# Tile 1's first half of W without A's columns, tile 0's h inside it, and warm-up products that read a constant: one change to a 16-tile LoRA kernel

## What is computed

```python
x = x + einsum('bct,bcd->bdt', x, weights[itok_B_0_15])
base_out = einsum('bti,oi->bto', x, W) + b
lora_h = einsum('bti,bir->btr', x, lora_As[itok_B_0_23])
lora_out = einsum('btr,bro->bto', lora_h, lora_Bs[itok_B_0_23])
x = x + base_out + lora_out * SCALING
```

## Time and profile before

| what | us |
|---|---|
| median of 3 runs (lowest, highest) | 84.74 (84.66, 84.76) |
| profiled execution, its own time | 84.83 |
| its span in the trace | 83.0 |
| PE busy (matmuls) | 78.5 (94%) |
| DVE (VectorE) busy | 60.1 (72%) |
| ACT (ScalarE) busy | 52.4 (63%) |
| POOL (GpSimd) busy | 33.5 (40%) |

### The profile page before, as it was taken

One profiled execution on the slowest core, in us unless ns is written; L12 is line 12 of the kernel. 1 busy time (PEld: TensorE's weight loads), 2 busy tenths in 40 slices (PEclk: granted clock), 3 DMA queues, 4 the chain that ended last, 5 costly groups with the idle time before them and its releaser, 6 DMA issues.

```text
span 83.0 us, 2012 instructions
## 1 busy us (share of the span) xinstructions
PE 78.5 (94%) x524; PEld 71.2 (86%) x524; DVE 60.1 (72%) x158; ACT 52.4 (63%) x180; POOL 33.5 (40%) x75
## 2 busy tenths in 40 slices
PE   4999599999999999999999999999999999999970
PEld 2376498899999999999999999999999999999950
DVE  2049595877879787777878787978777777869560
ACT  1555758866666675958666666667685867665520
POOL 6108843744443517080715344352608071304300
PEclk9999999999999999999999999999999999999999
DMA  2899899998476766877668778667774626130334
GB/s 24 279 349 317 202 253 216 355 252 247 142 233 197 255 197 241 198 230 196 183 205 200 210 190 241 173 238 184 236 179 155 167 91 175 30 118 0 126 126 126
DMA packets 16141, 16.07 MB, mean 193 GB/s; under 512 B 10241, under 2 KB 10626, under 8 KB 16130
## 3 DMA queue, kind: packets, MB, share of 16 engines
q1 hardware_dynamic: 14016, 11.67, 46.9%
q0 software_dynamic: 1248, 4.06, 18.6%
q10 hardware_dynamic: 866, 0.21, 1.1%
HBM read 11.74 MB, written 4.19 MB: 192 GB/s over the span
## 4 chain that ended last, share of the span: by engine, by line
PE 85%; DMA 6%; ACTq 3%; ACT 2%; DVE 1%; issue 1%; DVEq 0%
PE z_ps L565 58%; PE z_ps L602 9%; DMA a_raw<-in_lora_a 6%; PE y_ps L617 4%; PE y_ps L615 4%; PE y_ps L613 4%; PE ht_ps L589 2%; ACTq L326 1%; PE ht_ps L652 1%; PE z_ps L597 1%; DVE y_sb L552 1%; ACT L320 1%; ACTq L316 1%; ACT a_sb L391 0%; ACTq L317 0%
## 5 line engine op out<-in xcount | busy, mean ns | idle before, releaser
L565 PE MATMUL z_ps<-wa,x_hi 128*128 128x288 f32 (+2 forms) x240 | 50.1, 301 | 0.0
L565 PEld LDWEIGHTS z_ps<-wa,x_hi 128*128 128x128 f32 x240 | 38.0, 188 | 1.8 <-issue 0.5
L565 PE MATMUL z_ps<-wa,x_lo 128*128 128x288 f32 (+2 forms) x120 | 35.3, 295 | 0.0
L565 PEld LDWEIGHTS z_ps<-wa,x_lo 128*128 128x128 f32 x120 | 22.6, 188 | 0.0
L303 POOL CAST m_hi<-m_raw 128x128 fp32r<-128x128 f32 x16 | 4.8, 301 | 35.3 <-ACT m_raw L340 35.3
L294 POOL DMA_INDIRECT b_raw<-in_lora_b,b_index_slot x16 | 16.8, 1048 | 4.4 <-POOL b_index_slot L292 4.4
L384 ACT CAST z_hi<-z_ps 128x256 fp32r<-128x256 f32 x31 | 10.1, 376 | 10.2 <-PE z_ps L602 10.1
L487 DVE TENSOR_TENSOR z_lo<-z_ps,z_hi 128x256 fp32r<-128x256 f32 x31 | 11.8, 420 | 6.3 <-ACT z_hi L384 6.3
L340 ACT COPY m_raw<-w_raw 32x32 f32 x64 | 13.8, 216 | 1.8 <-DVE w_raw L519 0.9
L446 DVE TENSOR_TENSOR x_lo<-x_raw,x_hi 128x512 fp32r<-128x512 f32 x14 | 9.7, 690 | 3.7 <-ACT x_hi L352 3.7
L467 DVE TENSOR_TENSOR b_lo<-b_raw,b_hi 128x512 fp32r<-128x512 f32 x15 | 10.4, 691 | 0.5
(11 more groups left out here) (58 smaller groups left out, 76.7 us busy)
## 6 DMA issues: line engine op xcount, KB each, us to landing
out<-y_sb SPq DMA_DIRECT2D x15, 256.0 KB, 2.4
x_raw<-in_xt SPq DMA_DIRECT2D x14, 256.0 KB, 3.2
a_raw<-in_lora_a SPq DMA_DIRECT2D x60, 32.0 KB, 2.9
first_sb<-in_first SPq DMA_DIRECT2D x2, 384.0 KB, 3.9
first_sb<-in_first SPq DMA_DIRECT2D x3, 256.0 KB, 4.8
b_raw<-in_lora_b,b_index_slot POOLq DMA_INDIRECT x16, 4.0
bias_sb<-in_bias SPq DMA_DIRECT2D x1, 256.0 KB, 4.3
a_raw<-in_lora_a ACTq DMA_DIRECT2D x4, 32.0 KB
```

The lines of the kernel that those rows point to most:

```text
L565: done = nc.tensor.matmul(target, (x_lo if lo_x else x_hi)[s][:, k, :], moving(lo_w), start=first and not lo_x and not lo_w, stop=last and ...
```

## The change

Five things change together. (1) The warm-up products read the program's constant of one (set up in the preamble) instead of a tile that VectorE clears, so they wait for nothing; the last has 384 columns in place of 256. (2) A is laid out on the host and in `a_raw` as [r][k], k innermost. Tile 0's h then reads its stationary operand straight from `a_raw` with a step of four elements, and the ScalarE copy is gone; but `round_a` and `rest_a` of every tile now read `a_raw` with that step too. (3) Tile 1 treats A as the last tile does: none beside half 0, 64 columns beside half 1. (4) Half 0 of tile 1 runs right after tile 0's chunks with waits cut finer, tile 0's h comes after its third chunk, and ScalarE and VectorE take W's last chunk ahead of tile 1's A. (5) `load_a(3)` waits for the end of tile 0's h on TensorE; and later tiles wait for z of the tile two back one half at a time.

```diff
-    WARM_UP = (512,) * 8 + (256,)
+    WARM_UP = (512,) * 8 + (384,)
...
-        a_raw = [sb(f"a_raw{s}", [P, J, KC, R], F32) for s in range(NA)]
-        a0_sb = sb("a0_sb", [P, KC, JR], F32)
+        a_raw = [sb(f"a_raw{s}", [P, J, R, KC], F32) for s in range(NA)]
...
+        def a0_chunk(k):
+            return a_raw[0][:, :, :, k:k + 1].rearrange("p j r a -> p (j r a)")
...
         def a_half(u, half):
-            return a_raw[u % NA][:, half * HJ:(half + 1) * HJ, :, :].rearrange("p j k r -> p k j r")
+            return a_raw[u % NA][:, half * HJ:(half + 1) * HJ, :, :].rearrange("p j r k -> p k j r")
+        WITH_A = {1: 1, LAST: 0}
         def a_place(u, half, lo):
-            row, at = (0, A_AT[1] + half * AC) if u == LAST else (half, A_AT[u % 2])
+            row, at = (WITH_A[u], A_AT[1] + half * AC) if u in WITH_A else (half, A_AT[u % 2])
...
                 if u == NA:
-                    sp.wait_ge(a0_ready, 1)
+                    sp.wait_ge(main_done, 1)
...
             round_x1(0)
-            act.wait_ge(a_loaded[0], 16 * J)
-            act.copy(a0_sb[:, :, :].rearrange("p k (j r) -> p k j r", j=J),
-                     a_raw[0][:, :, :, :].rearrange("p j k r -> p k j r")).then_inc(a0_ready, 1)
             round_x1(1)
+            round_w(KC - 1)
             round_a(1)
-            round_w(KC - 1)
...
             rest_x1(1)
+            rest_w(3)
             rest_a(1)
-            rest_w(3)
...
-            pe.wait_ge(zeros_ready, 1)
             for columns in WARM_UP:
+                nc.tensor.matmul(ht_ps[:, 0:columns], nc.const_aps.tensor(1.0, (P, P), BF16),
+                                 nc.const_aps.tensor(1.0, (P, columns), BF16), start=True, stop=True)
...
+            def half_chunk(u, k, half, parts=(HH, HL, LH)):
+                n = HALF + 2 * AC if half == WITH_A[u] else HALF
+                return products(u, k, z_ps[1][:, half, 0:n], lambda lo: wa[:, k, lo, half, AC:AC + n], parts)
             def main_chunk(u, k, half):
...
+                if k == 0 and half == 1:
+                    pe.wait_ge(z_ready, 2 * (u - 1))
...
             def wait_main(u):
-                pe.wait_ge(x_ready, u + (u > 1))
-                pe.wait_ge(a_ready, 2 * u - (u == 1))
-                if u >= 2:
-                    pe.wait_ge(z_ready, 2 * (u - 1))
+                pe.wait_ge(x_ready, u + 1)
+                pe.wait_ge(a_ready, 2 * u)
+                pe.wait_ge(z_ready, 2 * (u - 1) - 1)
...
+            def first_h():
+                pe.wait_ge(a_loaded[0], 16 * J)
+                for k in range(KC):
+                    last = nc.tensor.matmul(ht_ps[0:JR, 0:P], a0_chunk(k), x0_chunk(k), start=k == 0,
+                                            stop=k == KC - 1, skip_group_check=True)
+                last.then_inc(main_done, 1)
+            pe.wait_ge(x_hi_ready, 1)
+            for k in range(2):
+                pe.wait_ge(w_ready, k + 1)
+                half_chunk(1, k, 0, (HH, HL))
+            pe.wait_ge(x_ready, 1)
+            for k in range(2):
+                half_chunk(1, k, 0, (LH,))
+            pe.wait_ge(x_hi_ready, 2)
+            pe.wait_ge(w_ready, 3)
+            half_chunk(1, 2, 0, (HH, HL))
+            pe.wait_ge(x_ready, 2)
+            half_chunk(1, 2, 0, (LH,))
+            first_h()
+            pe.wait_ge(w_hi_ready, KC)
+            half_chunk(1, 3, 0, (HH, LH))
+            pe.wait_ge(w_ready, KC)
+            half_chunk(1, 3, 0, (HL,))
+            pe.wait_ge(a_ready, 2)
+            half_chunk(1, 0, 1)
+            half_chunk(1, 1, 1)
+            lora(0, 0)
+            lora(0, 1)
+            half_chunk(1, 2, 1)
+            half_chunk(1, 3, 1).then_inc(main_done, 1)
...
-        "lora_a": lora_a.reshape(-1, KC, P, R).transpose(0, 2, 1, 3),
+        "lora_a": lora_a.reshape(-1, KC, P, R).transpose(0, 2, 3, 1),
```

More of the change, by code:

```diff
@@ L26, in lora_residual_program @@
     C, S0, _ = w0.shape
-    SLOTS, _, _, R = lora_a.shape
+    SLOTS, _, R, _ = lora_a.shape
     T = KC * P
@@ L70, in lora_residual_program @@
         own_mask0 = sb("own_mask0", [JR, J, C], F32)
-        zeros = sb("zeros", [P, P], BF16)
         scratch = sb("scratch", [P, 1], F32)
@@ L119, in lora_residual_program @@
         last_part_stored = sem("last_part_stored")
-        zeros_ready = sem("zeros_ready")
         ident_zero = sem("ident_zero")
@@ L139, in lora_residual_program @@
         a_ready = sem("a_ready")
-        a0_ready = sem("a0_ready")
         b_hi_ready = sem("b_hi_ready")
@@ L179, in a_half @@
         def a_half(u, half):
-            return a_raw[u % NA][:, half * HJ:(half + 1) * HJ, :, :].rearrange("p j k r -> p k j r")
+            return a_raw[u % NA][:, half * HJ:(half + 1) * HJ, :, :].rearrange("p j r k -> p k j r")
+        WITH_A = {1: 1, LAST: 0}
         def a_place(u, half, lo):
-            row, at = (0, A_AT[1] + half * AC) if u == LAST else (half, A_AT[u % 2])
+            row, at = (WITH_A[u], A_AT[1] + half * AC) if u in WITH_A else (half, A_AT[u % 2])
             return wa[:, :, lo, row, at:at + AC].rearrange("p k (j r) -> p k j r", j=HJ)
         def h_of(u):
-            if u == LAST:
-                return z_ps[1][:, 0, HALF:HALF + 2 * AC].rearrange("p (a j r) -> p a j r", a=2, j=HJ)
+            if u in WITH_A:
+                return z_ps[1][:, WITH_A[u], HALF:HALF + 2 * AC].rearrange("p (a j r) -> p a j r", a=2, j=HJ)
             at = H_PS[u % 2]
@@ L230, in load_a @@
                     slot = sp.snap(adapters[j], min_val=0, max_val=SLOTS - 1)
-                    sp.dma_start(a_raw[u % NA][:, j:j + 1, :, :].rearrange("p j k r -> p j (k r)"),
-                                 lora_a[bass.ds(slot, 1)].rearrange("s p k r -> p s (k r)")
+                    sp.dma_start(a_raw[u % NA][:, j:j + 1, :, :].rearrange("p j r k -> p j (r k)"),
+                                 lora_a[bass.ds(slot, 1)].rearrange("s p r k -> p s (r k)")
                                  ).then_inc(a1_half_loaded[j // HJ] if u == 1 else a_loaded[u % NA], 16)
@@ L317, in _ @@
             act.dma_start(ids_p_sb[:, :], ids_of_p).then_inc(ids_p_loaded, 16)
-            act.wait_ge(zeros_ready, 1)
-            act.copy(scratch[:, :], zeros[:, 0:1])
+            act.copy(scratch[:, :], nc.const_aps.tensor(1.0, (P, 1), BF16))
             adapters0 = [act.alloc_register(f"adapter0_{j}") for j in range(J)]
@@ L325, in _ @@
                 slot = act.snap(adapters0[j], min_val=0, max_val=SLOTS - 1)
-                act.dma_start(a_raw[0][:, j:j + 1, :, :].rearrange("p j k r -> p j (k r)"),
-                              lora_a[bass.ds(slot, 1)].rearrange("s p k r -> p s (k r)")
+                act.dma_start(a_raw[0][:, j:j + 1, :, :].rearrange("p j r k -> p j (r k)"),
+                              lora_a[bass.ds(slot, 1)].rearrange("s p r k -> p s (r k)")
                               ).then_inc(a_loaded[0], 16)
@@ L430, in _ @@
         def _(dve):
-            nc.vector.memset(zeros[:, :], 0.0).then_inc(zeros_ready, 1)
             nc.vector.memset(own_mask[:, :], 0.0).then_inc(mask_zero, 1)
@@ L567, in products @@
+            HH, HL, LH = (0, 0), (0, 1), (1, 0)
+            def products(u, k, target, moving, parts=(HH, HL, LH)):
+                for part in parts:
+                    done = nc.tensor.matmul(target, (x_hi, x_lo)[part[0]][u % 2][:, k, :], moving(part[1]),
+                                            start=k == 0 and part == HH, stop=k == KC - 1 and part == parts[-1],
                                             skip_group_check=True)
                 return done
+            def half_chunk(u, k, half, parts=(HH, HL, LH)):
+                n = HALF + 2 * AC if half == WITH_A[u] else HALF
+                return products(u, k, z_ps[1][:, half, 0:n], lambda lo: wa[:, k, lo, half, AC:AC + n], parts)
@@ L570, in main_chunk @@
             def main_chunk(u, k, half):
                 s = u % 2
[L572 to L577, removed]
+                if k == 0 and half == 1:
+                    pe.wait_ge(z_ready, 2 * (u - 1))
                 return products(u, k, z_ps[s][:, half, 0:NW],
-                                lambda lo: wa[:, k, lo, half, MOV[s]:MOV[s] + NW], k == 0, k == KC - 1)
+                                lambda lo: wa[:, k, lo, half, MOV[s]:MOV[s] + NW])
@@ L649, in _ @@
                 first_chunk(k)
[L650 to L656, removed]
+            def first_h():
[28 more added lines that the diff above has]
+            half_chunk(1, 3, 1).then_inc(main_done, 1)
+            for u in range(2, LAST):
                 wait_main(u)
                 main_chunk(u, 0, 0)
[L660 to L664, removed]
+                main_chunk(u, 0, 1)
+                mix(u - 2)
+                transpose_h(u - 1)
+                main_chunk(u, 1, 0)
                 main_chunk(u, 1, 1)
@@ L673, in last_chunk @@
             def last_chunk(k, half):
-                n = (HALF + 2 * AC, HALF)[half]
```

(5 more changed lines are left out.)

## The result

| | before | changed |
|---|---|---|
| median of four runs, us | 84.75 | 87.0 |
| lowest and highest | 84.66, 84.77 | 86.46, 87.09 |
| profiled execution (span) | 84.83 (83.0) | 87.09 (85.4) |

What follows compares the result with a forecast made beforehand. PE looked saturated, busy 94%, with VectorE's masked h arriving at the same moment, without slack. Terms -0.65 + 0.22 + 0.1 + 2.64 = +2.3 us on 84.83 gave 87.1, as median 87.0; range 83.8 to 88.3.

Steps and rivals of the forecast that it cites:

- The read with a step: VectorE's rests of A read lone elements four apart: 110 ns more per rest, between nothing and 133.
- No slack in the loop: Two longer rests stand ahead of the masked h on VectorE: 0.22 us per tile, 12 x 0.22 = 2.64.
- The signs: Expected profile: tile of 4.70, PE idle some 0.2 us before LoRA products, DVE busier by 3.3, PE's busy time hardly changed.
- The start: Filled 0.88 us gap: tile 2 at about 14.1, tile 1's LoRA products 0.65 earlier; step adds 0.22 and 0.1.
- The warm-up: Earlier warm-up products before tile 0: counted at nothing, since tile 0's third chunk still waits for VectorE.
- The wait that is moved: A of tile 3 loads after tile 0's h, from 11.18; ScalarE waits for its landing, 15.65 at median.
- The bias behind A of tile 3: Bias queued behind those loads is needed a tile later; counted at nothing.
- rival with a free read: Stepped read of A costs nothing, so the start's 0.65 stays: 84.1, at best 83.8; chance 0.25.
- the late A: A of tile 3 lands late and the read is free: with 4.0 from issue, +0.4, 85.1; chance 0.06.
- the unmoved start: Tile 2 still begins at 15.00, the loop still pays: 84.74 + 2.64 = 87.4; inside the forecast's range, no separate chance.

Runs made afterwards that it cites:

- runs of two: Changed kernel with A of tiles 1 to 15 in runs of 2 neighbours instead of 16, masked h behind the rests; 84.84 us, measured once.
- masked h first: Changed kernel with VectorE's masked h put ahead of the two rests of A in tiles 2 to 14; 84.24 us, 0.9935 of the kernel before.
- both cures: Changed kernel with A of tiles 1 to 15 in runs of 16 and the masked h ahead of the rests of A; 84.18 us.
- both cures, four buffers: Changed kernel with A of tiles 1 to 15 in runs of 16, masked h ahead of the rests, and a fourth buffer for A; 84.12 us.
- layout undone: Changed kernel with A of tiles 1 to 15 laid out as before, only tile 0's A in the new layout; 84.48 us, 0.9956 of the kernel before.

## Why the prediction was right

The total, 87.0, was met, and the mechanism was the one forecast. Two terms were off, the start by 0.28 and the loop by 0.34, and cancelled; that the total fits so closely is luck, that the kernel is slower through VectorE's longer rests is not.

- *The read with a step.* Forecast 110 ns per rest, measured 377 - 284 = 93, or 0.73 ns for each of 128 elements, not the nearly full second element time that I took. The estimate from the Trainium skill (Vector Engine (DVE) Microarchitecture Reference, "Measured stream behaviour on trn2"), 87 ns, was nearer, although its price is for hops of 4 KiB and here a step is 16 bytes; its pairs at full rate agree with the 284 ns of runs of two.
- *No slack in the loop.* Forecast 12 x 0.22 = 2.64; measured 2.30, of which 0.30 fall in the first of the twelve periods (below) and 0.18 in each of the others. Two rests of 93 ns make 0.19: nearly their whole length passes through.
- *The signs.* A tile of 4.68 and a DVE busier by 2.8 us came near the 4.70 and 3.3 forecast. But PE showed no idle time ahead of the LoRA products, and its busy time rose by 3.3 us: the wait stands on PEld, 0.18 a tile, with the masked h as releaser.
- *The start.* Forecast -0.33 with the step's share in it, measured -0.05. Several steps failed here. The warm-up was counted at nothing, but tile 0's chunks ended at 9.17, not 8.51: PE's pace rose late in this execution (last section). Tile 0's h took 1.22, not 1.09: its weight loads read the stepped layout in 207 ns, before 136, and I had taken nothing. So M and z of tile 0 came later, z's rest at 14.36 and not 13.6 (before 14.10), and tile 2 began at 14.93, not 14.1. The loads of h, before and changed, and z's rest in the changed kernel:

```profile
L652 PEld LDWEIGHTS ht_ps<-first_sb,a_sb 128*64 128x64 f32 x8 | 0.8, 136 | 1.3 <-ACT a_sb L391 1.3
```

```profile
L652 PEld LDWEIGHTS ht_ps<-first_sb,a_raw 128*64 128x64 f32 x8 | 1.0, 207 | 0.1
```

```profile
14.36 0.76 DVE L484 TENSOR_TENSOR z_lo<-z_ps,z_hi 128x256 fp32r<-128x256 f32 x2 [0.78 <-ACT z_hi L385]
```

- *The wait that is moved.* In this execution the step failed in its reason. A of tile 3 was not what ScalarE waited for: its issues ran from 11.90, later than the 11.18 forecast, yet its casts show no wait, as the first two timelines below say. In two quicker starts (masked h first, both cures) ScalarE did wait for it, until 15.64 and 15.71, near the 15.65 forecast.
- *A of tile 4*, behind it in the same queue, has no term in the forecast. ScalarE waited 0.26 for it (the third timeline), the second rest of that tile started behind the late cast, and the first period of the loop took 4.78 where the others took 4.67: some 0.11 of the 2.30 go with this wait and not with the rests alone.

```profile
11.90 1.90 SPq L233 DMA_DIRECT2D a_raw<-in_lora_a  x4
```

```profile
15.63 0.76 ACT L367 CAST wa<-a_raw 128x128 fp32r<-128x128 f32 x2
```

```profile
20.78 0.74 ACT L367 CAST wa<-a_raw 128x128 fp32r<-128x128 f32 x2 [0.26 <-DMA a_raw<-in_lora_a]
```

- *The bias behind A of tile 3*, which I had counted at nothing, did wait in the quicker starts (0.75 us with the masked h first, 0.33 with both cures).
- The sum with measured terms: 84.83 - 0.05 + 2.30 = 87.08; the profiled execution took 87.09.

The rival with a free read fell with the 377 ns; the late A and the unmoved start fell as causes of the loss, since undoing the layout alone gave 84.48. Of the late A the 0.11 above is left, and the rival of the unmoved start describes this start well: z of tile 0 came no earlier and tile 2 began 0.07 earlier, although the reason, the late rise of the pace, stands in no rival.

## What to carry to other kernels

A layout is paid for by every reader, not only by the one it was made for: one copy of 0.4 us was saved once, and the two rests in each of twelve tiles became longer by 0.09 each. Before trusting a saturated engine, look in one late period at who arrives first at each wait; where the other engine arrives at the same moment, put the work that nobody waits for behind the work that somebody does. Here moving one line was worth as much as the whole new layout had cost.

## What was unexpected

The pace of TensorE rose at different times in executions with the same warm-up. The granted clock on the page is 9 tenths or more in every slice, but PE's timeline of the changed kernel, in two stretches, shows two paces within tile 0's chunks:

```profile
4.97 1.49 PE L643 MATMUL z_ps<-first_sb 128*128 128x256 f32 x3
```

```profile
6.85 2.32 PE L643 MATMUL z_ps<-first_sb 128*128 128x256 f32 x10
```

With 634 ns for one in the first stretch and 379 in the second (the longest and the median of that line), the starts are (1.49 - 0.634) / 2 = 0.43 us and (2.32 - 0.379) / 9 = 0.216 us apart: a factor of two, the levels of 1.2 and 2.4 GHz. With the masked h first and the same warm-up the chunks took 4.02 in place of 4.63:

```profile
4.49 4.02 PE L643 MATMUL z_ps<-first_sb 128*128 128x256 f32 x16
...
16.92 0.27 PE L600 MATMUL z_ps<-b_hi,ht_sb 128*128 128x256 f32 x1
```

There tile 1's LoRA products stood at 16.92, 0.5 earlier than in the changed kernel. The profiled executions of all six kernels with the new start fall in two groups (us):

| kernel | tile 0's chunks end | tile 2 begins | LoRA products of tile 1 |
|---|---|---|---|
| both cures, four buffers | 8.40 | 14.14 | 16.61 |
| masked h first | 8.51 | 14.45 | 16.92 |
| both cures | 8.35 | 14.57 | 17.04 |
| runs of two | 9.09 | 14.83 | 17.30 |
| changed | 9.17 | 14.93 | 17.41 |
| layout undone | 9.26 | 15.01 | 17.47 |

Where the chunks end near the 8.51 that the prediction took, tile 2 begins 0.4 to 0.9 earlier than the 15.00 before (0.9 was forecast); where the pace rises late, next to nothing of the gain is left. That the three early ones all have the masked h first is taken for chance here, since that edit moves nothing ahead of tile 2; it was not tested. So the start's gain comes and goes with the execution, which fits the spread of the changed kernel's four runs (86.46 to 87.09). Whether the new warm-up makes a late rise more likely is open: in the three profiled executions with the old one the chunks ended at 8.36 to 8.56. That the filled idle time is what used to hide a late rise was argued, not shown.
